# Three turning PSUM banks for scores, row maxima and outputs in two 16-head attentions, and a causal scale moved into Q

## What is computed

```
# first layer: causal, K and V rounded to 8 bits
q, k, v = heads(x @ w_attn + b_attn + 2 * (x @ la @ lb))     # 16 heads of 16
k, v = fake_quant(k), fake_quant(v)      # (clip(round(t / s + z), 0, 255) - z) * s
scores = where(causal, q @ k.T / sqrt(16), -inf)
out = softmax(scores) @ v

# second layer: all positions
q, k, v = heads(x @ Wq.T), heads(x @ Wk.T), heads(x @ Wv.T)
out = (softmax(q @ k.T * 256 ** -0.5) + relative_bias) @ v
```

## Time and profile before

| | us |
|---|---|
| median of 3 executions | 2634.31 |
| lowest, highest | 2629.5, 2645.07 |
| the profiled execution, own time | 2638.67 |
| its span in the profile | 2637.0 |
| causal attention, from its first score product to its last output | about 108 to 426 |
| paired attention, the same | about 1084 to 1520 |

### The profile page before, as it was taken

One profiled execution on the slowest core, in us unless ns is written; L12 is line 12 of the kernel. 1 busy time (PEld: TensorE's weight loads), 2 busy tenths in 40 slices (PEclk: granted clock), 3 DMA queues, 4 the chain that ended last, 5 costly groups with the idle time before them and its releaser, 6 DMA issues. The chain is left out here.

```text
span 2637.0 us, 39124 instructions
## 1 busy us (share of the span) xinstructions
PE 2015.1 (76%) x14401; PEld 1034.8 (39%) x14401; DVE 1599.9 (61%) x3002; ACT 1080.3 (41%) x1890; POOL 769.7 (29%) x987
## 2 busy tenths in 40 slices
PE   6698887888479989699999953777386693388991
PEld 3333334323332226133333322444152362277981
DVE  3767673486347875678888545997474306365442
ACT  3367775143103435477777722222220312144330
POOL 3122220253113440746655201332000000422225
PEclk9789997898689999799999976687698796599996
DMA  5100001000100002100000033000110200343113
GB/s 183 60 22 22 24 16 30 0 1 2 35 0 1 1 13 84 64 31 32 29 33 28 11 124 111 2 2 2 38 64 32 70 0 5 125 171 109 50 45 104
DMA packets 79900, 117.12 MB, mean 44 GB/s; under 512 B 17815, under 2 KB 57763, under 8 KB 78181
## 3 DMA queue, kind: packets, MB, share of 16 engines
q1 hardware_dynamic: 71125, 102.72, 11.4%
q0 software_dynamic: 3664, 9.32, 1.2%
q10 hardware_dynamic: 4928, 2.62, 0.4%
HBM read 80.23 MB, written 34.14 MB: 43 GB/s over the span
## 5 line engine op out<-in xcount | busy, mean ns | idle before, releaser
L1181 DVE TENSOR_REDUCE a_mx<-a_SM 128x2 f32<-128x1024 f32 x256 | 299.7, 1216 | 65.6 <-PE a_SM L1054 65.3
L1164 ACT ACTIVATE a_P<-a_ST 128x512 f32<-128x512 f32 x512 | 292.6, 598 | 105.6 <-PE a_ST L1080 104.5
L876 ACT ACTIVATE a_P<-a_ST,a_scale 128x512 f32<-128x512 f32 (+3 forms) x384 | 206.3, 588 | 84.0 <-PE a_ST L788 82.5
L891 DVE TENSOR_REDUCE a_mx<-a_SM 128x2 f32<-128x1024 f32 (+1 forms) x192 | 176.2, 951 | 66.8 <-PE a_SM L753 37.8
L1080 PE MATMUL a_ST<-a_Q,a_K 98*128 98x512 bf16 (+1 forms) x512 | 187.1, 392 | 22.2 <-DMA a_Q<-a_MS 12.7
L1099 PE MATMUL a_OP<-a_P,a_V 128*32 128x256 f32 (+1 forms) x1792 | 157.9, 424 | 4.1 <-ACT a_P L1164 0.7
L723 POOL TENSOR_SCALAR_AFFINE_SELECT a_P<-a_P 128x128 f32<-128x128 f32 (+1 forms) x256 | 77.1, 306 | 242.7 <-ACT a_P L876 241.5
L788 PE MATMUL a_ST<-a_Q,a_K 50*128 50x512 bf16 (+3 forms) x384 | 119.3, 358 | 24.1 <-ACT a_P L876 23.6
L3178 POOL CAST work<-work 128x512 bf16<-128x512 f32 x92 | 73.9, 841 | 209.2 <-PE experts_py L3267 194.9
L3347 DVE TENSOR_TENSOR experts_hl<-work 128x512 bf16<-128x512 f32 x92 | 83.8, 969 | 80.3 <-POOL work L3178 80.3
L3251 PE MATMUL experts_ph<-experts_x,experts_w1h 128*128 128x256 bf16 x736 | 126.8, 276 | 3.4 <-DVE experts_x L3341 1.7
(11 more groups left out here) (578 smaller groups left out, 4497.6 us busy)
## 6 DMA issues: line engine op xcount, KB each, us to landing
work<-L_ffn_W SPq DMA_DIRECT2D x16, 1024.0 KB, 6.0
conv_tab<-dft_tables SPq DMA_DIRECT2D x8, 1024.0 KB, 4.9
bias_hankel<-bias_rows SPq DMA_DIRECT2D x16, 448.0 KB, 6.0
a_K<-a_k_parts SPq DMA_DIRECT2D x96, 64.0 KB
a_Q<-a_q_parts SPq DMA_DIRECT2D x96, 64.0 KB
expert_rows<-zeros SPq DMA_DIRECT2D x1, 5888.0 KB, 23.0
experts_x<-expert_rows SPq DMA_DIRECT2D x23, 256.0 KB, 3.0
expert_results<-params SPq DMA_DIRECT2D x23, 256.0 KB, 2.2
```

The costliest lines, as they stand in the source:

```text
L876: act.activation(Pr[:, s % 2, u, j, c0:N], ST[:, u, c0:N], ACT.Exp, scale=kscale[:, 0:1]).then_inc(exp_done, 1)
L891: dve.tensor_reduce(mx[:, g % 2, qt, k0 // N, :], SM[:, c % 2, :, 0:kn], AX.X, ALU.max).then_inc(mx_read, 1)
L1164: act.activation(Pr[:, s % 2, u, j, :], ST[:, (4 * s + x) % 2, :], ACT.Exp, scale=scale).then_inc(exp_done, 1)
L1181: dve.tensor_reduce(mx[:, g % 2, qt, k0 // N, :], SM[:, c % 2, :, :], AX.X, ALU.max).then_inc(mx_read, 1)
```

## The change

Four edits in two stages and one beside them.

1. `ST` (two banks) and `AUX` (one) become `ring` (three banks). A list `order` holds every score tile, R and O in TensorE's program order; the use number i gets bank i mod 3. `wait_for_bank` makes each use wait only until the use three turns back has been emptied, whatever kind it was. This is done in both attentions.
2. The waits of R and O on all former uses of `AUX` go; they too call `wait_for_bank`.
3. In the causal stage the exponential takes no scale operand any more.
4. Instead the projections multiply Q by `kscale` as ScalarE takes it out of PSUM, and the bias of Q is multiplied by `kscale` once (`bq`, one small VectorE instruction, and one wait of ScalarE for it).

```
 def quantized_projections
-                        act.activation(dst, pm[:, m % 6, :], ACT.Identity, bias=bqk[:, w, c:c + 1]).then_inc(ev, 1)
+                        if w:
+                            act.activation(dst, pm[:, m % 6, :], ACT.Identity, bias=bqk[:, 1, c:c + 1]).then_inc(ev, 1)
+                            continue
+                        act.wait_ge(scaled, 1)
+                        act.activation(dst, pm[:, m % 6, :], ACT.Identity, bias=bq[:, c:c + 1], scale=kscale[:, 0:1]).then_inc(ev, 1)
...
                 dve.tensor_scalar(kscale[:], qs[:, 0:1], scale, None, ALU.mult).then_inc(inv, 1)
                 dve.wait_ge(inv, 2)
+                dve.tensor_scalar(bq[:], bqk[:, 0, :], kscale[:, 0:1], None, ALU.mult).then_inc(scaled, 1)

 def causal_attention
+    BANKS = 3
+    order = [("rows", 0), ("rows", 1)]
+    for s in range(NG * ns):
+        for x in range(4):
+            if x == 1 and event(rows_at, s):
+                order.append(("rows", 2 * event(rows_at, s)[0] + event(rows_at, s)[1]))
+            if x == 3 and event(outputs_at, s):
+                order.append(("outputs", 2 * event(outputs_at, s)[0] + event(outputs_at, s)[1]))
+            order.append(("scores", 4 * s + x))
+    order.append(("outputs", 2 * NG - 1))
+    turn = {use: i for i, use in enumerate(order)}
+
+    def bank(use, n):
+        return turn[use, n] % BANKS
...
-        SM, ST = st.ps("SM", [P, 2, 2, N]), st.ps("ST", [P, 2, N])
-        OP, AUX = st.ps("OP", [P, N]), st.ps("AUX", [P, N])
+        SM, OP, ring = st.ps("SM", [P, 2, 2, N]), st.ps("OP", [P, N]), st.ps("ring", [P, BANKS, N])
...
+        emptied = {"scores": exp_done, "rows": rows_copied, "outputs": y_done}
+
+        def wait_for_bank(pe, use, n):
+            if turn[use, n] >= BANKS:
+                former, m = order[turn[use, n] - BANKS]
+                pe.wait_ge(emptied[former], m + 1)
...
                 def rows(g, half):
                     pe.wait_ge(neg_ready, 2 * g + half + 1)
-                    if taken.outputs:
-                        pe.wait_ge(y_done, taken.outputs)
-                    if taken.rows:
-                        pe.wait_ge(rows_copied, taken.rows)
-                    taken.rows += 1
+                    wait_for_bank(pe, "rows", 2 * g + half)
+                    out = ring[:, bank("rows", 2 * g + half), :]
... (outputs the same)
-                    if m >= 2:
-                        pe.wait_ge(exp_done, m - 1)
+                    wait_for_bank(pe, "scores", m)
...
-                        act.activation(Pr[:, s % 2, u, j, c0:N], ST[:, u, c0:N], ACT.Exp,
-                                       scale=kscale[:, 0:1]).then_inc(exp_done, 1)
+                        act.activation(Pr[:, s % 2, u, j, c0:N], ring[:, bank("scores", 4 * s + x), c0:N], ACT.Exp).then_inc(exp_done, 1)
```

More of the change, by code:

```diff
@@ L787, in scores @@
                     r = slice(u * WD, u * WD + KX)
-                    last = pe.matmul(ST[:, u, c0:N], Ks[r, g % slots, k * P:(k + 1) * P],
+                    last = pe.matmul(ring[:, bank("scores", m), c0:N], Ks[r, g % slots, k * P:(k + 1) * P],
                                      Qs[r, g % slots, qh * N + c0:(qh + 1) * N], start=True, stop=True)
@@ L811, in outputs @@
                     pe.wait_ge(ot_done, 2 * g + half + 1)
-                    if taken.outputs:
-                        pe.wait_ge(y_done, taken.outputs)
-                    if taken.rows:
-                        pe.wait_ge(rows_copied, taken.rows)
-                    taken.outputs += 1
+                    wait_for_bank(pe, "outputs", 2 * g + half)
+                    out = ring[:, bank("outputs", 2 * g + half), :]
                     for t in range(QTN):
-                        last = pe.matmul(AUX[:, t * P:t * P + 2 * (HD + 1)], OT[:, t * P:(t + 1) * P],
+                        last = pe.matmul(out[:, t * P:t * P + 2 * (HD + 1)], OT[:, t * P:(t + 1) * P],
                                          sel[:].rearrange("p u d -> p (u d)"), start=True, stop=True)
@@ L862, in rows @@
                         act.wait_ge(rows_ld[e % 2], 32 * (e // 2))
-                    act.copy(MS[:, e % 2, :], AUX[0:4, :]).then_inc(rows_copied, 1)
+                    act.copy(MS[:, e % 2, :], ring[0:4, bank("rows", e), :]).then_inc(rows_copied, 1)
                 for e in range(2):
@@ L909, in result @@
                     dve.wait_ge(out_ready, 2 * g + half + 1)
-                    out = AUX[:].rearrange("p (t n) -> p t n", t=QTN)[:, :, 0:2 * (HD + 1)].rearrange("p t (u d) -> p t u d", u=2)
+                    out = ring[:, bank("outputs", 2 * g + half), :].rearrange("p (t n) -> p t n", t=QTN)[:, :, 0:2 * (HD + 1)].rearrange("p t (u d) -> p t u d", u=2)
                     dve.reciprocal(rc[:], out[:, :, :, HD]).then_inc(rc_done, 1)
@@ L963, in place, with bank @@
         return divmod(g, HP)
+    BANKS = 3
+    order = [("rows", 0)]
+    for s in range(NG * ns):
+        for x in range(4):
+            if x == 3 and event(rows_at, s):
+                order.append(("rows", 2 * event(rows_at, s)[0] + event(rows_at, s)[1]))
+            order.append(("scores", 4 * s + x))
+        if event(outputs_at, s):
+            order.append(("outputs", 2 * event(outputs_at, s)[0] + event(outputs_at, s)[1]))
+    order.append(("outputs", 2 * NG - 1))
+    turn = {use: i for i, use in enumerate(order)}
+    def bank(use, n):
+        return turn[use, n] % BANKS
     with Stage(nc, name) as st:
@@ L1059, in rows @@
                     pe.wait_ge(neg_ready, 2 * g + half + 1)
-                    if taken.outputs:
-                        pe.wait_ge(y_done, taken.outputs)
-                    if taken.rows:
-                        pe.wait_ge(rows_copied, taken.rows)
-                    taken.rows += 1
+                    wait_for_bank(pe, "rows", 2 * g + half)
+                    out = ring[:, bank("rows", 2 * g + half), :]
                     for t in range(QTN):
-                        last = pe.matmul(AUX[0:4, t * P:(t + 1) * P], MR[:, g % 2, half * QTN + t, :], K.identb[:],
+                        last = pe.matmul(out[0:4, t * P:(t + 1) * P], MR[:, g % 2, half * QTN + t, :], K.identb[:],
                                          start=True, stop=True)
```

23 lines of the change are left out of this document (9 added, 14 removed).

## The result

The changed kernel takes 2605.28 us, median of 4 executions (2602.35 to 2610.83). The kernel before took 2636.19 beside it (4 executions). The ratio is 0.9883, 95% interval 0.9849 to 0.9918, so it is faster by 30.9 us, 22 to 40. I had forecast 2618 with a range of 2606 to 2634.

What follows compares the result with a forecast made beforehand. No engine is full; in the causal stage TensorE and ScalarE hold each other up. Gains 14.3, 0.4 and 1.5 make 16.2: 2638.67 - 16.2 + 0.1 = 2622.6; that profile was 4.4 above the median, so 2618, range 2606 to 2634.

Steps and rivals of the forecast that it cites:

- The exponentials: Causal stage: a 128x512 exponential without the scale operand takes 598 ns instead of 685.
- A: Whole kernel, as worked out: 2618 us, own range 2611 to 2626; chance 0.47.
- First half group: Causal group, R at 292.27 to R at 302.18: the next R comes 0.57 us earlier.
- the failed step: Causal first half: VectorE, reading two chunks of n4, is late next, so R gains 0.57 us, not 0.86.
- Second half group: Causal group, 302.18 to 310.98: the `OT` copy, values, O, the result and R come 0.49 us earlier.
- Beginning and end of the stage: Causal stage: 1.5 us put on the last 25 us, where TensorE waits for exponentials at both ends of each step.
- rival C: Causal stage, 148 to 176 us: the slow stretch at 1.2 GHz, costing 7.5 us, may not come: 2611; chance 0.12.
- B: Causal group: VectorE's reads and ScalarE's copies are the chain, so 0.5 us per group, 8 us: 2626; chance 0.25.
- D: Causal loop: slower through more low-clock stretches, 7.5 us each, 2618 + 7.5 k; chance 0.06.
- E: Causal loop: s3 behind R waits 0.35 us for the copy to `MS`, 32 times, 11 us; at most 2645; chance 0.06.
- The paired stage: Paired attention: 0.15 us from the ring is given back at n0's wait for the row of maxima; taken as 0.
- The projections: Projections: a second column operand on each of 8 Q tiles costs 0 to 0.2 us, taken as 0.1.

Runs made afterwards that it cites:

- run with short maxima: From the changed kernel, VectorE takes the causal stage's maxima over half of each chunk's columns only; 2603.8 us, ratio 0.9837.
- copy later: From the changed kernel, ScalarE copies the finished outputs behind the second exponential of their step, not the first, causal stage only; 2629.11 us, ratio 0.996.
- copy first on the kernel before: From the kernel before, ScalarE copies the finished outputs ahead of the exponential of their step, nothing else; 2709.15 us in one execution.
- earlier loads: From the changed kernel, the paired attention's stack loads for the group after next are issued one step earlier; 2596.52 us, ratio 0.982.

## Why the prediction was wrong

**The exponentials** were right: 601 ns for the 598 that I took. The mechanism of A was right too: the ring takes TensorE's waits away and the shorter exponentials bring the copy of `OT` forward. What failed are three terms of the sum (the group, the end of the stage, the clock).

**First half group.** I had 0.57; it is 0.82. The values came 0.27 us earlier, against my 0.32. O starts 7.22 behind R instead of 8.16, 0.94 earlier, against my 0.86. I then took 0.29 off because VectorE would be late. This is the failed step. Its two reads started at 258.24, 5.54 behind R instead of 5.97: 0.43 earlier, where I had 0.29. It had 0.33 of idle time in hand, and 0.09 more, since the reciprocal starts ahead of the end of the instruction in front of it (261.12 against 261.04 + 0.17). That makes 0.85, and R follows. My own figures were off as well: 297.95 + 2.35 + 0.6 is 300.90, not 300.97. The run with short maxima shows that VectorE holds back only 0.07 of a first half.

**Second half group.** 0.68 against 0.49. The mechanism was right, the copy of `OT` stands ahead of the values and comes earlier. It starts 4.64 behind R (266.43 in the profile of the changed kernel, R at 261.79) instead of 5.37, 0.73 earlier. The mis-sized term is the work of ScalarE ahead of it. I counted two exponentials as shorter, 0.2 us. In the changed kernel six stand without a pause ahead of the copy (263.80, x6). In the kernel before the same six stood so:

```profile
304.22 2.19 ACT L876 ACTIVATE a_P<-a_ST,a_scale 128x128 f32<-128x128 f32 x4 [0.22 <-PE a_ST L788]
306.61 1.05 ACT L876 ACTIVATE a_P<-a_ST,a_scale 128x512 f32<-128x512 f32 x2 [0.19 <-PE a_ST L788]
```

The first of the six starts at the same distance from R in both kernels, 2.04 and 2.01 us. From there to the copy it was 3.33 and is 2.63: the pause of 0.19 is gone, and six exponentials that are 0.087 shorter give 0.52. Scale alone took 0.45 of this half, ring alone 0.38, where I had 0.2 and 0.25. Together the group lost 1.50 instead of 1.06, over the stage 21.8 instead of 14.7 (14.3 and 0.4).

**Beginning and end of the stage.** I put 1.5 us on the end, without a working; it gave 4.2. The end is all exponentials and waits for them, so it should have been worked out. The first half I put at nothing; it gave 1.8 here, of which up to 1.2 depends on when the clock comes back (6.84 or 8.05 by profile).

**The clock** is the largest error of judgement. I gave rival C 0.12, on the ground that from 176 to 398 the same pauses stood at clock 1.00. Four profiles of that kernel hold 8.2 to 18.2 us of it, the five with the new causal stage 0 to 2.3. C's price, 7.5, was near the 8.2 of that profile. One stretch in one profile looked like an accident and was a property of the kernel. The four executions profiled of before are 2638.67 to 2646.74, mostly above the timed median, so in an ordinary execution this part is likely smaller than the 13.6 that they hold on average; how much of the 31 us it is there, no run shows. The Trainium skill ("TensorE: Matmul & The Clock Gate", on psum-queue depth-cycling) says that cycling through PSUM banks with frequent small idle times makes the clock swing. I had set its rule aside. The trace agrees for the kernel before (0.63 to 0.77 in the 20 us windows of its stretches), but the scale alone, with the same two banks, stood at 1.00 for 245.8 us, and the ring alone, with three, had four short drops. The rule did not tell where a given kernel stands.

**Rivals.** B, half of it, is out. D, more such stretches, did not come with this change but did with two others (copy later; copy first on the kernel before): the mechanism is real, I had only its sign for this change right. E: the new wait for the copy to `MS` is there, 0.35 us as worked out, but once a group (15 times, 5.3 us), not twice. It does not hold the group: ScalarE ran the copy to `MS` and the three exponentials behind it without a pause (254.40, x3), so not even the 0.08 that I had counted shows. The paired stage came out at nothing as forecast, and for the reason given: its half groups at full clock went from 12.83 to 12.63, and the wait for the row of maxima, which the earlier loads then removed, took it back. The projections: 779 ns for a Q tile with two operands, 92 more than with one, nothing on the stage that can be seen.

**What stays open.** Why the clock falls at one repeat of a group and not at the next, why it stays low for some 14 to 24 us in the kernel before and about 3.4 in most drops with three banks, and which of the two edits is what keeps it up in the changed kernel.

## What to carry to other kernels

Split a repeating group at the points where one engine lets the other go, and test each piece by moving one instruction one place: +0.50 and -0.50 us here showed which of the listed waits was a link of the chain, as neither busy shares nor the list itself do. When every instruction of a kind gets shorter, count all of them that stand between an engine's last pause and the event that others wait for, not only the nearest. Before pricing a stretch at low clock as an accident, profile the same kernel several times. In this kernel an edit that shortened pauses on TensorE was worth more than its pauses, and one that lengthened them cost several times as much: the same move of one copy was -12 us (-14.5 by the spans) with the ring and 62 to 70 more on the kernel before.

## What the runs showed of the hardware

- The granted clock depends on the rhythm of a kernel in a way that partly repeats: a drop in the same four groups in two profiles of the ring alone; one or two stretches of some 14 to 24 us at 0.50 inside the causal stage in each of four profiles of the kernel before; none in five profiles of the changed causal stage. The kernel before with the copy first stood between 0.50 and 0.76 in 14 of 15 windows of 20 us from 140 to 440 us, while TensorE read 91% busy from 260 to 420 (145.20 of 160).
- Two windows of 2 us with the same 14 matmuls and 1.37 us busy were followed by 1.00 once and by 0.53 once.
- A second column operand on an ACTIVATE (92 ns) cost about as much as the first (84 to 87): 779 and 687 ns with two and one on the Q tiles, 685 and about 600 with one and none on exponentials, all of 128x512.
- Exponentials in a row overlap: three of 601 ns took 1.66 us from start to end (254.40), so they started 0.53 apart.
- Halving the columns of VectorE's reductions took away 43% of their time (176 to 101 us), and changed the stage by about 1 us.
